# Value bias folded into the value weight, and the f1 bias products placed behind the first attention, in an attention and feed-forward kernel on one core

## Chip, cores and metric

One core of a Trainium2 chip runs the kernel. The metric is the device time of one execution in microseconds; less is better. Engines are named as in the profile: PE is TensorE (matmuls), DVE is VectorE, ACT is ScalarE, POOL is GpSimd, SP issues the loads and stores.

## What is computed

The input x is 8 batches of 512 rows of 256 numbers. The reference, cut down:

```python
x = x + attn_block(layernorm(x), ...)
x = x + ffn_block(layernorm(x), W_fc, ln_w, ln_b, W_proj)

# attn_block
x_norm = layer_norm(x, ln1_w, ln1_b)
Q = elu(x_norm @ q_w.T + q_b) + 1;  K = elu(x_norm @ k_w.T + k_b) + 1     # 64 features each
V = x_norm @ v_w.T + v_b
# causal, step by step in n: KV += k v^T ; Ks += k ; out = (q KV) / (q . Ks + 1e-6)
x = x + (attn @ o_w.T + o_b)
h = gelu(layer_norm(x, ln2_w, ln2_b) @ f1_w.T + f1_b)                      # 1024 wide
x = x + h @ f2_w.T + f2_b

# ffn_block: W_fc and W_proj are rounded to -1, 0, 1 by their mean absolute value
h = layernorm(gelu(x @ absmean(W_fc).T)) * ln_w + ln_b
return h @ absmean(W_proj).T
```

## The kernel before

**Precision.** Most products are made in fp32r from a high and a low part of each operand: hi x hi, hi x lo, lo x hi (split3). The high part is a copy on ACT (names ending in _hi), the low part a subtraction on DVE (_lo). wfc and wpj hold -1, 0, 1 and need no low part.

**One batch g** (T = 4 row tiles of 128, h or half = two of them, k = two column tiles of D = 256):

- ln1_stats, ln1_rstd (POOL), ln1_shift, u_norm: u, the normalised row. tu flips it (four 128x128 transposes per half) and u_hi, u_lo copy it to uT.
- qk_mm, then qk_max, qk_exp (its own ACT table), qk_sum, qk_hi, k_dup, qk_lo make q_stack, k_stack and k_lo. scores makes the causal blocks in three banks; ae_mask, ad_mask, af_mask multiply the diagonals; the parts go to ae, ad, af.
- v_mm multiplies uT by wvo, the product of v_w, o_w and ln1_w, so attend gives rows of the output projection at once. v has 258 columns: column 256 is one, so that attend sums up the denominator too. attend(g, t) starts each sum with ones_row x eps_row, which adds 1e-6 to the denominator and takes 1e-6 times the bias row from the others. attn_out divides and adds xa, which holds n1 (the row normalised for the inner residual) plus bo_b: POOL's n1o adds it.
- ln2, z2_norm, tz2, z2_hi, z2_lo; f1(g, m), m = 0..7, each 128 of the 1024 wide layer, gelu, h_hi, h_lo; f2(g, m) sums them up; y_sum.
- ln3, z3_norm, tz3, z3_hi, z3_lo; fc(g, t, c), gelu3; tr flips h3, g_hi and g_lo apply ln_w; proj; correct (POOL) and output; store.

**Order.** Each engine has its instructions written out as a list: first() for batch 0, step(g) for batches 1 to 5, last() for 6 and 7. A step interleaves work of batches g-1, g, g+1 and g+2. Engines run their lists in order and wait for each other by semaphores (pe.wait_ge and so on). Nothing reorders them, so a place in a list is a place in time.

**Set-up in first().** wqk and wvo are scaled by ln1_w. qkb multiplies ln1_b by the raw q and k weights; bvo makes the bias row of v and o, from the columns vb and ln1_b spread over 128 columns by wide_cols: bo_rows adds o_b to it (bo_b) and makes eps_raw, which eps_split and eps_lo turn into eps_row. f1b makes the bias of f1 from ln2_b: 16 products of one column each, into bank_y[0]; f1_bias_add adds f1_b, and gelu(0, 0) waits for that. abs_part(0..3), theta_sum, threshold and ternary make wfc and wpj from the raw weights. In SP's list the load of the raw fc waits for wf1_lo, and the load of the raw pj, into the place where f1_raw lay, waits for f1b:

```python
            sp.wait_ge(s["wf1_lo"], 4)
            sp.dma_start(fc_raw, fc_d).then_inc(s["fc_loaded"], 16)
            sp.wait_ge(s["f1b_done"], 1)
            sp.dma_start(pj_raw, pj_d).then_inc(s["pj_loaded"], 16)
```

Of the kernel before, what the change touches and what calls it, by code (L numbers as in the profile page):

```python
# [1301 lines left out]
```

## Time and profile before

| | |
|---|---|
| runs | 467.3, 467.65, 470.79 us, median 467.65 |
| profiled execution | 467.8 us, its span (first to last instruction) 465.8 us |
| PE busy | 448.6 us, 96% of the span |
| DVE, ACT, POOL busy | 369.0, 322.3, 187.5 us |
| mean granted clock of PE | 0.985 of full |

A share of busy time is a mean over the whole span. PE's matmuls overlap: the distance from one start to the next is what a matmul costs in a packed row, and is shorter than the duration of its record. A granted clock of 1.00 is 2.4 GHz and 0.50 is 1.2 GHz. Lines (L346) are those of the kernel before.

### The profile page before, as it was taken

How to read it: one execution, taken by the hardware profiler on the slowest of the kernel's cores; microseconds unless marked ns; L12 is line 12 of the kernel's file. 1: busy time of each engine (PE TensorE's matmuls, PEld its weight loads, DVE VectorE, ACT ScalarE, POOL GpSimd, SP SyncE). 2: the span in 40 equal slices, each digit the busy share in tenths (PEclk: the TensorE clock that was granted, in tenths of full speed). 3: DMA queues.
4: the chain of work that ended last, by engine and by line, in shares of the span. 5: the costliest groups of instructions: out<-in, count | busy, mean ns of one | idle time of the engine just before them, and what ended most of it. 6: DMA issues, size and time to landing. Idle time of an engine off the chain costs nothing.

```text
span 465.8 us, 8944 instructions
## 1 busy us (share of the span) xinstructions
PE 448.6 (96%) x3012; PEld 408.1 (88%) x3012; DVE 369.0 (79%) x1184; ACT 322.3 (69%) x606; POOL 187.5 (40%) x188
## 2 busy tenths in 40 slices
PE   4988999999999999999999999999999999999996
PEld 4876898889989999889989899889998999889875
DVE  6978969875898779985898868986898768767675
ACT  4976856988368864988468874788459793775262
POOL 3967025510565042640545123740545323540433
PEclk9977999999999999999999999999999999999999
DMA  7241000000020002000020002000020000000001
GB/s 236 117 181 45 1 2 1 1 23 2 1 68 2 25 0 69 2 23 1 2 68 2 24 0 70 0 24 2 1 68 2 23 1 15 9 2 24 0 23 46
DMA packets 10044, 14.08 MB, mean 30 GB/s; under 512 B 784, under 2 KB 9104, under 8 KB 9488
## 3 DMA queue, kind: packets, MB, share of 16 engines
q1 hardware_dynamic: 10000, 13.52, 8.6%
q8 instruction: 24, 0.39, 0.4%
q14 instruction: 20, 0.16, 0.1%
HBM read 9.32 MB, written 4.19 MB: 29 GB/s over the span
## 4 chain that ended last, share of the span: by engine, by line
PE 69%; issue 13%; POOL 6%; DVE 2%; ACT 1%; POOLq 0%; DVEq 0%; ACTq 0%
PE bank_f L415 10%; PE bank_p L445 10%; PE bank_f L203 5%; PE bank_f L204 5%; PE bank_f L205 5%; PE bank_y L204 5%; PE bank_y L203 5%; PE bank_y L205 5%; PE bank_y L429 4%; PE bank_a L203 3%; PE bank_a L205 3%; PE bank_a L204 3%; PE bank_a L211 2%; PE bank_f L211 1%; POOL rs L1155 1%
## 5 line engine op out<-in xcount | busy, mean ns | idle before, releaser
L1155 POOL TENSOR_TENSOR rs<-ve,neg_half 128x2 f32<-128x2 f32 x48 | 33.7, 701 | 227.3 <-DVE ve L846 225.5
L204 PE MATMUL bank_y<-wf_lo,h_hi 128*128 128x256 f32 x240 | 67.1, 280 | 0.0
L203 PE MATMUL bank_y<-wf_hi,h_hi 128*128 128x256 f32 x240 | 67.1, 279 | 0.0
L205 PE MATMUL bank_y<-wf_hi,h_lo 128*128 128x256 f32 x240 | 67.0, 279 | 0.0
L445 PE MATMUL bank_p<-wpj_t,g_hi 128*128 128x256 f32 x256 | 64.0, 286 | 0.3 <-DVE y_yc L1048 0.3
L445 PE MATMUL bank_p<-wpj_t,g_lo 128*128 128x256 f32 x256 | 62.4, 280 | 0.0
L1039 DVE SCALAR_TENSOR_TENSOR g_lo<-bank_y,vec,g_hi 128x256 fp32r<-128x256 f32 x128 | 54.9, 477 | 9.4 <-ACT g_hi L687 9.2
L687 ACT ACTIVATE g_hi<-bank_y,vec 128x256 fp32r<-128x256 f32 x128 | 52.5, 475 | 10.2 <-PE bank_y L429 8.2
L650 ACT ACTIVATE bank_f<-bank_f,f_bias 128x512 f32<-128x512 f32 x64 | 42.3, 660 | 23.7 <-PE bank_f L205 23.2
L415 PE MATMUL bank_f<-wfc_t,z3T_hi 128*128 128x512 f32 x128 | 53.9, 421 | 1.4 <-DVE z3T_lo L907 1.4
L203 PE MATMUL bank_f<-z2T_hi,wf_hi 128*128 128x512 f32 x128 | 53.3, 416 | 1.2 <-DVE z2T_lo L907 1.2
L907 DVE TENSOR_TENSOR h_lo<-bank_f,h_hi 128x512 fp32r<-128x512 f32 x60 | 41.2, 686 | 15.2 <-ACT h_hi L658 14.9
L678 ACT ACTIVATE h<-bank_f 128x512 f32<-128x512 f32 x64 | 38.3, 600 | 20.0 <-PE bank_f L415 19.8
L205 PE MATMUL bank_f<-z2T_hi,wf_lo 128*128 128x512 f32 x128 | 51.4, 402 | 0.0
L204 PE MATMUL bank_f<-z2T_lo,wf_hi 128*128 128x512 f32 x128 | 51.4, 402 | 0.0
L415 PE MATMUL bank_f<-wfc_t,z3T_lo 128*128 128x512 f32 x128 | 50.6, 396 | 0.0
L445 PEld LDWEIGHTS bank_p<-wpj_t,g_hi 128*128 128x128 f32 x256 | 48.1, 188 | 1.8 <-issue 0.5
L445 PEld LDWEIGHTS bank_p<-wpj_t,g_lo 128*128 128x128 f32 x256 | 48.3, 189 | 1.0
L203 PEld LDWEIGHTS bank_y<-wf_hi,h_hi 128*128 128x128 f32 x240 | 45.2, 188 | 1.1
L204 PEld LDWEIGHTS bank_y<-wf_lo,h_hi 128*128 128x128 f32 x240 | 45.1, 188 | 1.0
L205 PEld LDWEIGHTS bank_y<-wf_hi,h_lo 128*128 128x128 f32 x240 | 45.1, 188 | 0.0
L1025 DVE BATCH_NORM_STATS2 bn<-h 128x6 f32<-128x512 f32 x64 | 41.1, 681 | 1.6 <-ACT h L678 1.5
(293 smaller groups left out, 1209.5 us busy)
## 6 DMA issues: line engine op xcount, KB each, us to landing
out<-y_yc SPq DMA_DIRECT2D x16, 256.0 KB, 2.2
x_even<-in_x SPq DMA_DIRECT2D x8, 256.0 KB, 3.0
x_odd<-in_x SPq DMA_DIRECT2D x8, 256.0 KB, 3.1
h<-in_f SPq DMA_DIRECT2D x1, 1024.0 KB, 7.9
y_yc<-in_f SPq DMA_DIRECT2D x1, 1024.0 KB, 9.9
h<-in_fc SPq DMA_DIRECT2D x1, 1024.0 KB, 4.9
h<-in_pj SPq DMA_DIRECT2D x1, 1024.0 KB, 4.8
z<-in_wv SPq DMA_DIRECT2D x1, 256.0 KB, 4.0
```

The source lines that it names most:

```text
L203: pe.matmul(ps, w[0], r[0], start=start, stop=False, skip_group_check=skip)
L204: pe.matmul(ps, w[0], r[1], start=False, stop=False, skip_group_check=skip)
L205: return pe.matmul(ps, w[1], r[0], start=False, stop=stop, skip_group_check=skip)
L415: mm = pe.matmul(bank_f[c][:], z3T[part][:, k, t * P:(t + 1) * P], wfc[:, k, c * 512:(c + 1) * 512], start=(k == 0 and part == 0), stop=(k ...
L445: mm = pe.matmul(bank_p[:, t * D:(t + 1) * D], gr[part][:, (8 * g + 4 * h + q) % RG, i, t * P:(t + 1) * P], wpj[:, m, :], start=(m == 0 an ...
L650: act.activation(bank_f[m % 2][:], bank_f[m % 2][:], ACT.Gelu, bias=f1_bias[:, m:m + 1]).then_inc(s["h_gelu"], 1)
L678: act.activation(h3[:, t, c * 512:(c + 1) * 512], bank_f[c][:], ACT.Gelu).then_inc(s["h3_ready"], 1)
L687: act.activation(gr[0][:, n % RG, i, :], bank_y[q % 2][:, i * D:(i + 1) * D], ACT.Copy, scale=ln3w_c[:, m:m + 1]).then_inc(s["g_hi"], 1)
L907: dve.tensor_tensor(dst, b, hi.bitcast(F32), ALU.subtract).then_inc(s[ready], 1)
L1025: dve.bn_stats(bn[3][:, t, 6 * c:6 * c + 6], h3[:, t, c * 512:(c + 1) * 512]).then_inc(s["ln4_bn"], 1)
L1039: dve.scalar_tensor_tensor(gr[1][:, n % RG, i, :], bank_y[q % 2][:, i * D:(i + 1) * D], ln3w_c[:, m:m + 1], gr[0][:, n % RG, i, :].bitcast ...
L1155: pool.tensor_tensor(rs[n][:, 2 * h:2 * h + 2], ve[n][:, 2 * h:2 * h + 2], neg_half[:, 0:2], ALU.pow).then_inc(s[f"ln{n + 1}_rs"], 1)
```

## The change

The sum of a normalised row u is zero. If one is added to each element of u, its product with a matrix that has the same row b/D in each of its D rows is b. So the bias of v and o is put into wvo, and uT holds u + 1: u_hi copies with a bias of one, u_lo adds one before it subtracts. The added one also brings the column sums of the weights; for q and k, and within wvo, these are taken out again by less_w = ln1_b - ln1_w in the place of ln1_b. With the bias in v, attention's numerator holds it, and 1e-6 is added to the denominator by itself:

- ones_row, eps_row, eps_hi, eps_raw, bo_b, eps_split, bo_rows and eps_lo are gone, and the matmul ones_row x eps_row that began each attend.
- attn_out has a new step den = b[:, D] + 1e-6, and the reciprocal waits for it.
- n1o adds ob_b, as loaded. A new dcol makes less_w; qkb and wide_cols wait for it.
- wvo_hi is split: wvo_copy copies the raw product, then bvo, then wvo_add (DVE) scales it and adds the bias row, then wvo_hi and wvo_lo.
- f1b stands behind attend(0, 3), v_mm(0) behind scores(0), and the lists of all engines are written in another order.

```diff
-                    mm = pe.matmul(bank_a[0][:, 0:1], wqk_raw[:, k, :], ln1b_c[:, k:k + 1],
+                    mm = pe.matmul(bank_a[0][:, 0:1], wqk_raw[:, k, :], less_w[:, k:k + 1],
...
                 b = a_bank(g, (2, 0, 1, 2)[t])
-                pe.matmul(b[:, 0:VW], ones_row[:], eps_row[:], start=True, stop=False)
...
-                    mm = split3(b[:, 0:VW], w, [r[:, j, :] for r in v], False, j == t)
+                    mm = split3(b[:, 0:VW], w, [r[:, j, :] for r in v], j == 0, j == t)
...
-                qkb(); tu(0, 0); tu(0, 1); wvo_mm(); qk_mm(0); bvo(); v_mm(0, 0); v_mm(0, 1); scores(0); f1b()
-                attend(0, 0); attend(0, 1); attend(0, 2); tu(1, 0); attend(0, 3); tu(1, 1); tz2(0, 0); tz2(0, 1)
+                qkb(); tu(0, 0); tu(0, 1); wvo_mm(); qk_mm(0); bvo(); scores(0); v_mm(0, 0); v_mm(0, 1)
+                attend(0, 0); attend(0, 1); attend(0, 2); attend(0, 3); f1b(); tz2(0, 0); tz2(0, 1); tu(1, 0)
...
+            def wvo_copy():
+                act.wait_ge(s["wvo_done"], 1)
+                act.activation(wvo_raw.rearrange("p k d -> p (k d)"), bank_a[1][:], ACT.Copy).then_inc(s["wvo_copied"], 1)
+
             def wvo_hi():
...
+                act.wait_ge(s["wvo_sum"], 2)
+                act.activation(wvo[0][:].rearrange("p k d -> p (k d)"), bank_a[1][:], ACT.Copy).then_inc(s["wvo_hi"], 1)
...
-                act.activation(uT[0][:, :, 2 * h * P:(2 * h + 2) * P], by_k(a_bank(g, h)), ACT.Copy).then_inc(s["u_hi"], 1)
+                else:
+                    act.wait_ge(s["one_set"], 1)
+                act.activation(uT[0][:, :, 2 * h * P:(2 * h + 2) * P], by_k(a_bank(g, h)), ACT.Identity,
+                               bias=one[:]).then_inc(s["u_hi"], 1)
...
+            def wvo_add():
+
+                dve.wait_ge(s["bvo_done"], 1)
+                dve.wait_ge(s["vec_loaded"], 16)
+                for k in range(KD):
+                    dve.scalar_tensor_tensor(bank_a[1][:, k * D:(k + 1) * D], wvo_raw[:, k, :], ln1w_c[:, k:k + 1],
+                                             bank_q[:, 0:D], ALU.mult, ALU.add).then_inc(s["wvo_sum"], 1)
...
-                lo_part(uT[1][:, :, cols], by_k(a_bank(g, h)), uT[0][:, :, cols], "u_lo")
+                dve.scalar_tensor_tensor(uT[1][:, :, cols], by_k(a_bank(g, h)), 1.0, uT[0][:, :, cols].bitcast(F32),
+                                         ALU.add, ALU.subtract).then_inc(s["u_lo"], 1)
...
-                dve.reciprocal(rden[:, t:t + 1], b[:, D:D + 1]).then_inc(s["rden_ready"], 1)
+                dve.tensor_scalar(den[:, t:t + 1], b[:, D:D + 1], 1.0, ATTN_EPS, ALU.mult, ALU.add).then_inc(s["den_ready"], 1)
+                dve.wait_ge(s["den_ready"], 4 * g + t + 1)
+                dve.reciprocal(rden[:, t:t + 1], den[:, t:t + 1]).then_inc(s["rden_ready"], 1)
```

PE, the start of batch 0, before: bvo (bank_a<-z,xa and bank_a<-xa), v_mm (bank_y<-wvo, 24 rows), scores (q_stack), f1b (bank_y<-vec,h), the first attend.

```order
L236 MATMUL bank_a<-z,xa 128x256 x2
L236 MATMUL bank_a<-xa 128x256 x2
L203 MATMUL bank_y<-wvo_hi,uT_hi 128x256
L204 MATMUL bank_y<-wvo_lo,uT_hi 128x256
...
L311 MATMUL bank_f<-q_stack,k_stack 128x512
L312 MATMUL bank_f<-q_stack,k_lo 128x512
...
L245 MATMUL bank_y<-vec,h 128x1 x16
L346 MATMUL bank_p<-eps_row,ones_row 128x258
L203 MATMUL bank_p<-v_hi,ae_hi 128x258
```

The same place now; behind f1b (L243) stand tz2(0) (bank_f<-ident,z), tu(1) (bank_a<-ident,u) and theta_sum(0).

```order
L234 MATMUL bank_a<-z,xa 128x256 x2
L234 MATMUL bank_a<-xa 128x256 x2
L308 MATMUL bank_f<-q_stack,k_stack 128x512
...
L201 MATMUL bank_y<-wvo_hi,uT_hi 128x256
...
L201 MATMUL bank_p<-v_hi,ae_hi 128x258
...
L243 MATMUL bank_y<-vec,h 128x1 x16
L209 MATMUL bank_f<-ident,z 128x128 x8
L209 MATMUL bank_a<-ident,u 128x128 x8
L254 MATMUL bank_y<-abs_sum,mean_w 128x2
L201 MATMUL bank_f<-z2T_hi,wf_hi 128x512
```

v_mm moved behind scores, f1b behind the attends, tu(1) behind tz2(0), and the row with eps_row is gone.

ACT between the second layer norm of batch 0 and its first gelus, before: z2_norm, z2_hi, abs_part(2) and (3) (g_hi,abs_sum<-h), gelu with its table load (bank_f), h_hi.

```order
L558 ACTIVATE z<-xa,sh,rs 128x256 x2
L643 ACTIVATE z2T_hi<-bank_f 128x2x256 x2
L541 ACTIVATE g_hi,abs_sum<-h 128x1024 x2
L650 ACT_TABLE_LOAD
L650 ACTIVATE bank_f<-bank_f,f_bias 128x512
L658 ACTIVATE h_hi<-bank_f 128x512
```

And now:

```order
L546 ACTIVATE z<-xa,sh,rs 128x256 x2
L634 ACTIVATE z2T_hi<-bank_f 128x2x256 x2
L580 ACTIVATE uT_hi<-bank_a,one 128x2x256 x2
L529 ACTIVATE g_hi,abs_sum<-h 128x1024
L641 ACT_TABLE_LOAD
L641 ACTIVATE bank_f<-bank_f,f_bias 128x512
```

u_hi(1) came in ahead of abs_part(2), and abs_part(3) went behind the second gelu.

DVE in a middle batch, behind the second v_lo (v_lo<-bank_a), before: output (y_yc<-bank_p), ln3_shift(g, 1) (sh<-mv,rs), attn_out(g + 1, 0) and ln2_stats (bn<-xa), z3_lo.

```order
L907 TENSOR_TENSOR v_lo<-bank_a,v_hi 128x2x256
L1048 SCALAR_TENSOR_TENSOR y_yc<-bank_p,rs,y_yc 128x256 x2
L852 TENSOR_SCALAR sh<-mv,rs 128x1 x2
L968 RECIPROCAL rden<-bank_a 128x1
L971 SCALAR_TENSOR_TENSOR xa<-bank_a,rden,xa 128x256
L976 BN_STATS bn<-xa 128x6
L907 TENSOR_TENSOR z3T_lo<-bank_f,z3T_hi 128x2x256
```

And now:

```order
L896 TENSOR_TENSOR v_lo<-bank_a,v_hi 128x2x256
L841 TENSOR_SCALAR sh<-mv,rs 128x1 x2
L1040 SCALAR_TENSOR_TENSOR y_yc<-bank_p,rs,y_yc 128x256 x2
L958 TENSOR_SCALAR den<-bank_a 128x1
L960 RECIPROCAL rden<-den 128x1
```

The ln3_shift went ahead of output, and den stands ahead of each reciprocal.

## Rows read from the trace of the kernel before

**Rows 1.** The page, busy us of each engine, share of the span, instructions.

```profile
PE 448.6 (96%) x3012; PEld 408.1 (88%) x3012; DVE 369.0 (79%) x1184; ACT 322.3 (69%) x606; POOL 187.5 (40%) x188
```

**Rows 2.** Three stretches, one batch each: us, busy us (records) by engine, clock, loads.

```profile
236.26:289.53 53.27, 53.27 (x369) 48.98 (x369) 43.47 (x142) 38.77 (x73) 21.28 (x21) 1.00 0.07 22
```

**Rows 3.** TensorE's waits: us in total, times, longest.

```profile
PE bank_f L211 <- ACT z L558: 2.4, 1, 2.4
PE bank_f L415 <- DVE z3T_lo L907: 1.4, 1, 1.4
...
PE bank_a L346 <- DVE v_lo L907: 0.5, 1, 0.5
```

**Rows 4.** TensorE in order of time, two attends: start us, us, instruction.

```profile
286.88 0.28 PE L346 MATMUL bank_a<-eps_row,ones_row 128*128 128x258 f32 x1
287.00 0.29 PE L203 MATMUL bank_a<-v_hi,ae_hi 128*128 128x258 f32 x1
```

**Rows 5.** TensorE in order of time, batch 0.

```profile
15.28 1.03 PE L236 MATMUL bank_a<-xa 128*128 128x256 f32 x4
...
19.54 0.50 PE L311 MATMUL bank_f<-q_stack,k_stack 128*128 128x512 f32 x1
...
20.93 5.27 PE L245 MATMUL bank_y<-vec,h 128*128 128x1 f32 x32
26.11 0.55 PE L346 MATMUL bank_p<-eps_row,ones_row 128*128 128x258 f32 x1
...
32.20 0.60 PE L211 MATMUL bank_a<-ident,u 128*128 128x128 f32 x4
...
38.96 0.79 PE L203 MATMUL bank_f<-z2T_hi,wf_hi 128*128 128x512 f32 x1 [1.20 <-DVE z2T_lo L907]
...
43.74 0.28 PE L256 MATMUL bank_p<-abs_sum,mean_w 128*128 128x2 f32 x2
...
45.37 0.40 PE L203 MATMUL bank_f<-z2T_hi,wf_hi 128*128 128x512 f32 x1
```

**Rows 6.** Stretches of half a us: TensorE's granted clock is the third last number.

```profile
22.50:23.00 0.50, 0.50 (x5) 0.50 (x5) 0.50 (x3) 0.50 (x2) 0.29 (x1) 0.65 0.00 0
...
36.00:36.50 0.50, 0.04 (x1) 0.07 (x2) 0.50 (x2) 0.50 (x2) 0.50 (x2) 0.80 0.00 0
43.00:43.50 0.50, 0.50 (x3) 0.43 (x2) 0.25 (x1) 0.22 (x1) 0.50 (x1) 0.87 0.08 25
```

**Rows 7.** ACT in order of time, and the load of pj (us to landing).

```profile
39.31 1.06 ACT L541 ACTIVATE g_hi<-h 128x1024 fp32r<-128x1024 f32 x1
...
40.48 1.28 ACT L650 ACT_TABLE_LOAD   x1
41.92 0.66 ACT L650 ACTIVATE bank_f<-bank_f,f_bias 128x512 f32<-128x512 f32 x1 [0.17 <-PE bank_f L205]
...
h<-in_pj SPq DMA_DIRECT2D x1, 1024.0 KB, 4.8
```

**Rows 8.** DVE in a middle batch, and the f1 of TensorE behind it.

```profile
287.19 0.16 DVE L968 RECIPROCAL rden<-bank_a 128x1 f32<-128x1 f32 x1
287.38 0.48 DVE L971 SCALAR_TENSOR_TENSOR xa<-bank_a,rden,xa 128x256 f32<-128x256 f32 x1
...
290.19 0.69 DVE L907 TENSOR_TENSOR z3T_lo<-bank_f,z3T_hi 128x512 fp32r<-128x512 f32 x1 [0.22 <-ACT z3T_hi L669]
...
301.37 0.88 DVE L1039 SCALAR_TENSOR_TENSOR g_lo<-bank_y,vec,g_hi 128x256 fp32r<-128x256 f32 x2 [0.31 <-ACT g_hi L687]
302.27 0.69 DVE L907 TENSOR_TENSOR z2T_lo<-bank_a,z2T_hi 128x512 fp32r<-128x512 f32 x1
...
303.34 0.48 PE L203 MATMUL bank_f<-z2T_hi,wf_hi 128*128 128x512 f32 x1
```

**Rows 9.** ACT and TensorE ahead of the scores of a middle batch.

```profile
324.33 2.08 ACT L558 ACTIVATE xa<-x_even,sh,rs 128x256 f32<-128x256 f32 x4
...
325.27 0.40 PE L311 MATMUL bank_a<-q_stack,k_stack 128*128 128x512 f32 x1
```

More of the change, by code:

```diff
@@ L323, in v_mm @@
                     pe.wait_ge(s["u_lo"], h + 1)
-                    pe.wait_ge(s["wvo_lo"], 2)
+                    pe.wait_ge(s["wvo_lo"], 1)
                 for j in range(2):
@@ L690, in first @@
             def first():
-                tables(); wqk_hi(); u_norm(0, 0); u_norm(0, 1); u_hi(0, 0); u_hi(0, 1); ln3_hi(); wf1_hi(0)
-                wf1_hi(1); wvo_hi(); wf1_hi(2); qk_exp(0); wf1_hi(3); qk_hi(0); wf2_hi(0); k_dup(0); v_hi(0, 0)
-                n1(0); ad_hi(0); ae_hi(0); v_hi(0, 1); af_hi(0); eps_split(); u_norm(1, 0); wf2_hi(1); wf2_hi(2)
-                abs_part(0); u_norm(1, 1); u_hi(1, 0); abs_part(1); u_hi(1, 1); wf2_hi(3); z2_norm(0, 0)
-                z2_norm(0, 1); z2_hi(0, 0); z2_hi(0, 1); abs_part(2); abs_part(3); gelu(0, 0); h_hi(0, 0)
@@ new lines, in first @@
+                tables(); u_norm(0, 0); u_norm(0, 1); u_hi(0, 0); u_hi(0, 1); wqk_hi(); wf1_hi(0); wf1_hi(1)
+                ln3_hi(); wvo_copy(); wf1_hi(2); qk_exp(0); wf1_hi(3); qk_hi(0); wvo_hi(); k_dup(0); n1(0); af_hi(0)
+                ad_hi(0); v_hi(0, 0); ae_hi(0); v_hi(0, 1); wf2_hi(0); wf2_hi(1); u_norm(1, 0); wf2_hi(2); wf2_hi(3)
+                u_norm(1, 1); abs_part(0); abs_part(1); z2_norm(0, 0); z2_norm(0, 1); z2_hi(0, 0); z2_hi(0, 1)
+                u_hi(1, 0); u_hi(1, 1); abs_part(2); gelu(0, 0); h_hi(0, 0); gelu(0, 1); h_hi(0, 1); abs_part(3)
@@ L1051, in first @@
             def first():
-                consts(); ln1_stats(0, 0); ln1_stats(0, 1); ln1_shift(0, 0); u_odd(0, 0); ln1_shift(0, 1)
-                u_odd(0, 1); n1_ve(0); u_lo(0, 0); n1_shift(0); selectors(); u_lo(0, 1); wide_cols(); wqk_lo()
-                ln1_stats(1, 0); qk_bias_add(); qk_max(0); wvo_lo(); qk_sum(0); ln1_stats(1, 1); qk_lo(0)
-                v_lo(0, 0); ln3_lo(); n1_ve(1); ad_mask(0); ae_mask(0); bo_rows(); af_mask(0); ad_lo(0)
-                ln1_shift(1, 0); ae_lo(0); af_lo(0); eps_lo(); v_lo(0, 1); attn_out(0, 0); ln2_stats(0, 0)
@@ new lines, in first @@
+                consts(); ln1_stats(0, 0); ln1_stats(0, 1); dcol(); ln1_shift(0, 0); u_odd(0, 0); ln1_shift(0, 1)
+                n1_ve(0); u_odd(0, 1); u_lo(0, 0); wide_cols(); wqk_lo(); n1_shift(0); u_lo(0, 1); qk_bias_add()
+                ln1_stats(1, 0); qk_max(0); qk_sum(0); wvo_add(); selectors(); ln1_shift(1, 0); qk_lo(0); wvo_lo()
+                ln1_stats(1, 1); af_mask(0); ad_mask(0); ae_mask(0); af_lo(0); ad_lo(0); v_lo(0, 0); ae_lo(0)
+                v_lo(0, 1); attn_out(0, 0); ln2_stats(0, 0); attn_out(0, 1); ln1_shift(1, 1); attn_out(0, 2)
@@ new lines, in first @@
+                af_mask(1); ln1_stats(2, 1); h_lo(0, 7); n1_ve(2); af_lo(1); ae_lo(1); ad_lo(1); y_sum(0, 0)
+                ln3_stats(0, 0); y_sum(0, 1); v_lo(1, 0); ln3_stats(0, 1); ln3_shift(0, 0); v_lo(1, 1)
+                ln3_shift(0, 1); attn_out(1, 0); ln2_stats(1, 0); attn_out(1, 1); ln1_shift(2, 0); z3_lo(0, 0)
+                z3_lo(0, 1); ln2_stats(1, 1); attn_out(1, 2); ln2_var(1, 0); attn_out(1, 3); ln2_stats(1, 2)
+                ln2_shift(1, 0); ln2_stats(1, 3); ln2_var(1, 1); ln4_stats(0, 0); g_lo(0, 0, 0); ln2_shift(1, 1)
```

286 lines of the change are left out of this document (128 added, 158 removed).

## The prediction

> **What bounds the kernel now.** I read the busy line first, then three equal batches, TensorE's waits, the order in time of TensorE, and last what DVE, ACT and the loads do at the places that the change touches. TensorE is busy 96% of the span [rows 1]. In a middle batch it is busy 53.27 of 53.27 us with 369 matmul records, while DVE has 43.47 and ACT 38.77 [rows 2]: in batches 1 to 6 the time is the sum of TensorE's start-to-start distances. It waits only at the two ends and behind batch 0: for the first loads, 2.4 us for the second layer norm of batch 0, 1.4 us for the first z3 [rows 3]. So an edit pays if it takes matmuls out of the packed part, or if it shortens the start up to the point where the packed part begins. The profiled execution took 467.8 us for a span of 465.8, against a median of 467.65 of three runs (467.3 to 470.79), so savings in the span can be taken from the median as they are.
>
> **The epsilon products.** Each attend began with ones_row x eps_row, 128x258. In the packed part it starts at 286.88 and the next at 287.00: 0.12 us, although a record alone shows 0.28 [rows 4]. Four go in each of 8 batches. Those of batches 1 to 7: 28 x 0.12 = 3.4 us, all on the path. The four of batch 0 are in the start, below. Other matmuls only change places, and a packed engine pays the same sum for them.
>
> **What DVE gets for it.** Each attn_out has a den step of one column, then a wait, then the reciprocal. No such step is in the trace of before; the nearest is the reciprocal, 0.16 us busy and 0.19 to the step that waits for it [rows 8]. Bounds 0 to 0.48 (its 256-wide neighbour); I take 0.19, 0.76 per batch. DVE has 53.27 - 43.47 = 9.8 us of idle per batch, so the sum is covered, but the stretch from attn_out to z2_lo is nearly full: z2_lo ends at 302.96 and the f1 that waits for it starts at 303.34, cover 0.38 [rows 8]. The new order takes n1_ve, an ln1_shift and an ln3_shift out of that stretch, eight one-column steps that do not wait for one another; at half the reciprocal's 0.16 each, an estimate, that is some 0.7 us, so den is about paid back, while TensorE comes 4 x 0.12 = 0.48 earlier. DVE also waited 0.22 and 0.31 us for ACT in the stretch, time that can be used. I take no wait, with 0.36 us per batch (rival 2) as its bound. u_hi with a bias and u_lo with an added constant keep their shapes: nothing, hidden in ACT's and DVE's idle time.
>
> **The start, to f1(0,2), the first work after which TensorE of before never waits until f2 ends (45.37 [rows 5]).**
> a) v_mm(0) used to stand between bvo and scores(0), and filled the time from about 16.3 to 19.2 in which qk is made. Now wvo_hi and wvo_lo wait for bvo, so v_mm stands behind scores. TensorE is empty from 16.3 (bvo, [rows 5]) until qk_lo. qk_lo comes some 0.3 later than for the 19.54 of before, since wvo_add, selectors and a shift stand ahead of it on DVE: scores at 19.85.
> b) scores take 1.39 (19.54 to 20.93 [rows 5]), v_mm 24 x 0.12 = 2.9: 4.3 us at full clock. But TensorE is empty for 3.5 us before. In the trace the clock fell at 36.4, after a 2.4 us wait and a shorter one with only four transposes between, and was back at 43.1, 4.1 us after dense work began at 38.96 [rows 3, 5, 6]. So I take the clock as lost here as well, at 1.2 GHz for some 3.4 us of this work, which costs half of it: +1.7. v_mm ends at 25.85.
> c) The first attend waits for masks and v_lo: 0.5. Its 30 matmuls x 0.12 = 3.6 run at full clock, where before the clock had fallen at 22.8 in f1b, ahead of them [rows 6]. End of attention 30.0, against 32.2, the start of the tu behind it [rows 5].
> d) f1b comes now: 5.2 us (20.93 to 26.11 [rows 5]), one column each, to 35.2. It lies under the DVE-POOL-ACT chain of the second layer norm, which needed 3 us in before, 32.2 to 35.2; so f1b itself is late by some 2 us.
> e) Two things hang on f1b. The load of pj is issued behind it, as in before, and lands 4.8 us later [rows 7]: 40.1. ACT has abs_part(2), which reads it, ahead of gelu(0,0): 1.2 (39.31 to the table load at 40.48), the table load 1.3, gelu 0.7 [rows 7], h_hi and h_lo about the same each, 0.4 for the hand-overs: 5.0. f1(0,2) waits for h_lo(0,0): 45.1. On the other branch tz2, 16 transposes and theta start at 35.2, f1(0,0) near 39.1; the twelve matmuls of f1(0,0) and f1(0,1) took 4.8 in before (38.96 to 43.74 [rows 5]), and qk_mm 1.5 (to 45.37, less theta), which gives 45.4, or 43.5 if the 16 transposes bring the clock back earlier. I take the pj branch, 45.1; gain **0.3**, bounds -0.3 and +1.9 (clock kept).
>
> **Behind it.** theta_sum(1) moves from before f1(0,2) to behind it: -0.2. From f2's end of batch 0 to fc(0,0,1) before had the waits 0.5 and 1.4 [rows 3]; now the third attend stands ahead of tz3 and waits for the second v_lo. I add the same DVE steps in the new order, and come to waits of 0.6 and 0.9, but one fc less lies under them: -0.2. At the end fc(7,0,0), which filled the wait for the last tz3, stands behind it, and z3_lo behind output(6,1): -0.2. Sum 3.4 + 0.3 - 0.2 - 0.2 - 0.2 = **3.1 us**: span 462.7, profiled execution 464.7, median 464.5.
>
> **Rule and row.** In b) the trace of before has no single wait of 3.5 us in the middle of work, only two shorter ones. The Trainium skill (TensorE: Matmul & The Clock Gate, "HAM oscillation") says that waits between stretches of matmuls put the clock back to half each time, and that one should keep TensorE fed. That speaks against this change, which opens such a wait where there was none. By it b) stands, 464.5; if the short waits of the rows were needed together, 462.9. No row of before shows this wait alone. The same page (What's actually happening) has the clock follow how busy TensorE is; the row differs: from 22.5 to 23.0 TensorE was busy 0.50 of 0.50 us, in f1b, and the clock fell [rows 6].
>
> **Rivals.**
> 1. The clock is kept over the empty stretch: b) costs nothing, attention ends at 28.3, f1b 33.5, pj 38.4, f1(0,2) 43.5, gain 1.9 instead of 0.3: **462.9**. For: scores start soon after. Against: the length of the gap. Chance 0.24.
> 2. DVE closes the ring in each batch: den's 0.76 is not paid back and z2_lo is late by 0.76 + 0.48 - 0.38 - 0.5 = 0.36, six times 2.2 us: **466.7**. For: cover of 0.38. Against: 9.8 us of idle. Chance 0.15.
> 3. The other side: ACT now has n1(g+1), 2.08 us, ahead of qk_hi and k_dup, where it stood behind k_dup (324.33, just as k_dup ended). scores started at 325.27, so cover was 0.96 [rows 9]. qk_exp goes ahead of h_hi(4), and f2 pieces ahead of scores, and by my sum of the new order about 0.5 us of cover is left. If those moves don't help, scores wait 2.08 - 0.96 = 1.1 us in each of six batches, 6.7 us: **471.2**, over before by 3.5. It turns slower than before from 0.52 us per batch on. Chance 0.07.
> 4. The change doesn't do what it says: a start of 258 columns taken out only lets the next one wait for its weights, and nothing of the 3.4 comes back: **467.9**. Against: the records follow at 0.12 with their loads beneath. Chance 0.04.
>
> **How the numbers follow.** Forecast 0.50, rivals 0.24, 0.15, 0.07 and 0.04. The range runs from 462.2 (rival 1 with the small losses gone) to 467.0 (rival 2); outside are rival 3, rival 4 and the ends, under 0.2. One per cent, 4.7 us, is about what this measurement can tell from no change: faster by more is 462.97 or less. Rival 1 lies on that line, 0.16 of its 0.24; the forecast gives 0.08: faster 0.24. Slower 0.05 from rival 3, the rest 0.71 within.
>
> **What would show it.** Right: no ones_row records; a middle batch of 52.8 us with TensorE busy throughout; an empty TensorE of about 3.5 us before scores(0) and half clock after it; f1b between attend(0,3) and tz2(0,0); abs_part(2) waiting for the pj load, near 40; f1(0,2) near 45. Wrong: a batch of 53 us or more (rivals 2 to 4, by the wait that stands at f1, scores or nowhere), or f1(0,2) near 43.5 at full clock. A clock lost for longer, or the wait for pj growing with its load, would move the start by more than my bounds.

## The result, and the profile after

The changed kernel takes 463.83 us, the median of 11 runs (462.61 to 464.79), against 469.58 for 11 runs of the kernel before (467.3 to 471.42): a ratio of 0.9881, 95% interval 0.9859 to 0.9904. The first three runs of before, on which the prediction rests, had a median of 467.65; it forecast 464.5. The time is 0.7 us off. The gain is further off: 3.1 us was forecast, 4.7 us lie between the spans of the two profiled executions (465.8 and 461.1), and 5.75 between the two medians of 11. The part in the packed batches is the one that was forecast. The rest came in the start, for which 0.3 us had been put down.

The page of the changed kernel, busy us by engine [rows 1], and a middle batch, from f1(4,0) to f1(5,0), in the columns of [rows 2]:

```profile
PE 441.1 (96%) x2980; PEld 399.3 (87%) x2980; DVE 369.7 (80%) x1212; ACT 321.1 (70%) x603; POOL 185.7 (40%) x188
```

```profile
247.02:299.81 52.79, 52.79 (x368) 48.23 (x366) 43.74 (x148) 38.66 (x74) 21.23 (x21) 1.00 0.07 21
```

A batch takes 52.79 us where it took 53.27: 0.48 less, four times 0.12, with TensorE busy throughout as before. The 32 records of ones_row are gone, and nothing has taken their place in the packed part.

TensorE in order of time in batch 0, the rows that answer to [rows 5]:

```profile
14.93 1.03 PE L234 MATMUL bank_a<-xa 128*128 128x256 f32 x4
20.30 0.50 PE L308 MATMUL bank_f<-q_stack,k_stack 128*128 128x512 f32 x1 [4.34 <-DVE k_lo L896]
...
26.86 0.36 PE L201 MATMUL bank_p<-v_hi,ae_hi 128*128 128x258 f32 x1 [0.63 <-DVE v_lo L896]
...
30.53 3.63 PE L243 MATMUL bank_y<-vec,h 128*128 128x1 f32 x32
34.44 0.84 PE L209 MATMUL bank_f<-ident,z 128*128 128x128 f32 x4 [0.28 <-ACT z L546]
...
38.42 0.48 PE L201 MATMUL bank_f<-z2T_hi,wf_hi 128*128 128x512 f32 x1
...
43.59 0.50 PE L201 MATMUL bank_f<-z2T_hi,wf_hi 128*128 128x512 f32 x1 [0.70 <-DVE h_lo L896]
```

The empty stretch is there, 4.34 us long. scores(0) start at 20.30, the first attend at 26.86, attention ends at 30.53, and f1b stands where the prediction put it. But it takes 3.63 us instead of 5.27 [rows 5]. The last row is f1(0,2): 43.59, where before had 45.37, and it waits 0.70 us for h_lo.

The granted clock at the same places (third last number of a row, as in [rows 6]):

```profile
21.00:21.50 0.50, 0.50 (x5) 0.50 (x4) 0.50 (x2) 0.00 (x0) 0.50 (x2) 0.63 0.00 0
24.50:25.00 0.50, 0.50 (x6) 0.50 (x6) 0.00 (x0) 0.16 (x1) 0.50 (x2) 0.96 0.00 0
31.00:31.50 0.50, 0.50 (x7) 0.50 (x6) 0.43 (x3) 0.50 (x1) 0.00 (x0) 1.00 0.00 0
34.50:35.00 0.50, 0.50 (x4) 0.38 (x4) 0.46 (x3) 0.28 (x1) 0.50 (x1) 0.79 0.00 0
38.00:38.50 0.50, 0.50 (x6) 0.50 (x4) 0.20 (x1) 0.45 (x2) 0.50 (x2) 0.80 0.52 213
```

A stretch with 0.63 has 0.13 us at full and the rest at half. So behind the empty stretch the clock is at half (1.2 GHz) from 21.1 to 24.5, 3.4 us, as forecast. It is at full (2.4 GHz) in all of f1b, falls at 34.8, and is back at 38.2, just ahead of f1(0,0). Read in the same way, it was at half in before from 22.7 to 29.5 and from 36.3 to 43.1, 6.8 us each time.

**Where the 4.7 us lie**, as distances between the same instructions in the two traces:

| stretch | before | after | gain | forecast |
| --- | --- | --- | --- | --- |
| start of the span to f1(0,2) | 45.37 | 43.59 | 1.78 | 0.3 |
| f1(0,2) to f1(1,0) | 44.91 | 45.08 | -0.17 | 0.08 (0.48 - 0.2 - 0.2) |
| five middle batches | 266.33 | 263.92 | 2.41 | 2.4 |
| f1(6,0) to the end of the span | 109.19 | 108.51 | 0.68 | 0.28 (0.48 - 0.2) |

The waits behind the start, first of before, then of after:

```profile
72.20 0.39 PE L346 MATMUL bank_a<-eps_row,ones_row 128*128 128x258 f32 x1 [0.49 <-DVE v_lo L907]
...
443.28 0.50 PE L415 MATMUL bank_f<-wfc_t,z3T_hi 128*128 128x512 f32 x1 [1.41 <-DVE z3T_lo L907]
```

```profile
70.57 0.39 PE L201 MATMUL bank_a<-v_hi,ae_hi 128*128 128x258 f32 x1 [0.49 <-DVE v_lo L896]
...
72.67 0.39 PE L201 MATMUL bank_a<-v_hi,ae_hi 128*128 128x258 f32 x1 [0.74 <-DVE v_lo L896]
...
436.42 0.66 PE L209 MATMUL bank_f<-ident,z 128*128 128x128 f32 x4 [0.76 <-ACT z L546]
437.57 0.50 PE L410 MATMUL bank_f<-wfc_t,z3T_hi 128*128 128x512 f32 x1 [0.49 <-DVE z3T_lo L896]
```

The third attend of batch 1 waits 0.74 us for the second v_lo, which is new. The 1.41 us wait for z3T_lo in before lay at 443.28, in batch 7, and not behind batch 0, where the prediction used it.

In a middle batch DVE and ACT stand to TensorE like this; the rows of the first block answer to [rows 8], those of the second to [rows 9]:

```profile
283.90 0.15 DVE L958 TENSOR_SCALAR den<-bank_a 128x1 f32<-128x1 f32 x1
284.08 0.17 DVE L960 RECIPROCAL rden<-den 128x1 f32<-128x1 f32 x1
...
298.90 0.69 DVE L896 TENSOR_TENSOR z2T_lo<-bank_a,z2T_hi 128x512 fp32r<-128x512 f32 x1 [0.41 <-ACT z2T_hi L634]
...
299.81 0.48 PE L201 MATMUL bank_f<-z2T_hi,wf_hi 128*128 128x512 f32 x1
```

```profile
322.05 0.63 ACT L598 ACTIVATE k_stack<-k_stack 64x512 fp32r<-64x512 f32 x1
...
323.13 0.39 PE L308 MATMUL bank_a<-q_stack,k_stack 128*128 128x512 f32 x1
```

A den step costs 0.18 us to the reciprocal (0.19 taken). k_dup ends at 322.68, 0.45 us ahead of the scores that need it (0.5 forecast). z2_lo ends at 299.59, 0.22 ahead of f1.

### The profile page after: what moved, and what is told of

The parts are those of the page before. It is cut to its first block, busy times and chain, and to the rows that moved or that the text cites. A ratio compares the mean times of both kernels' runs of the same rounds, so it can differ in the third digit from the quotient of the medians.

```text
span 461.1 us, 8907 instructions
## 1 busy us (share of the span) xinstructions
PE 441.1 (96%) x2980; PEld 399.3 (87%) x2980; DVE 369.7 (80%) x1212; ACT 321.1 (70%) x603; POOL 185.7 (40%) x188
## 4 chain that ended last, share of the span: by engine, by line
PE 84%; DVE 6%; issue 4%; POOL 2%; ACT 2%; DMA 1%; DVEq 0%; POOLq 0%; ACTq 0%
PE bank_f L410 13%; PE bank_p L440 12%; PE bank_y L201 6%; PE bank_y L202 6%; PE bank_y L203 6%; PE bank_f L201 6%; PE bank_f L203 6%; PE bank_y L424 6%; PE bank_f L202 6%; PE bank_a L201 4%; PE bank_a L203 4%; PE bank_a L202 4%; PE bank_a L209 3%; PE bank_f L209 2%; PE bank_a L308 1%
## 5 line engine op out<-in xcount | busy, mean ns | idle before, releaser
L669 ACT ACTIVATE h<-bank_f 128x512 f32<-128x512 f32 x64 | 38.7, 607 | 21.2 <-PE bank_f L410 21.1
L202 PEld LDWEIGHTS bank_y<-wf_lo,h_hi 128*128 128x128 f32 x240 | 45.1, 188 | 0.9
L201 PEld LDWEIGHTS bank_y<-wf_hi,h_hi 128*128 128x128 f32 x240 | 45.1, 188 | 0.9
L203 PEld LDWEIGHTS bank_y<-wf_hi,h_lo 128*128 128x128 f32 x240 | 45.1, 188 | 0.0
```

The source lines that it names most:

```text
L201: pe.matmul(ps, w[0], r[0], start=start, stop=False, skip_group_check=skip)
L202: pe.matmul(ps, w[0], r[1], start=False, stop=False, skip_group_check=skip)
L203: return pe.matmul(ps, w[1], r[0], start=False, stop=stop, skip_group_check=skip)
L669: act.activation(h3[:, t, c * 512:(c + 1) * 512], bank_f[c][:], ACT.Gelu).then_inc(s["h3_ready"], 1)
```

## The experiments

Twelve kernels. A batch is the distance from one f1(g,0) to the next; f1(0,2) is read from TensorE's order in time. Since the moment at which the clock falls shifts from run to run (the mean clock of the runs of after is 0.985 to 0.993, of before 0.982 to 0.989), the start is read with its clock beside it, and what is said of the clock below holds for the one execution of each kernel that was traced.

### The products of ones, put back

eps_row holds zeros here; the 1e-6 still comes from the den step.

```
+ if g:
+     pe.matmul(b[:, 0:VW], ones_row[:], eps_row[:], start=True, stop=False)
- mm = split3(..., j == 0, j == t)
+ mm = split3(..., j == 0 and g == 0, j == t)
```

> The changed kernel with one 128x258 product of ones by zeros put back at the head of each attend of batches 1 to 7 (the epsilon still comes from the den step). Theory: each costs 0.12 us of the packed TensorE, 28 of them 3.4 us; a middle batch takes 53.27 us again instead of 52.79, and the span is 464.5 instead of 461.1. Rival (the product was hidden, and the time went elsewhere): batch stays at 52.79 and the span at 461.1.

Measured: 468.79 us, ratio to before 1.0 (0.9983 to 1.0017), span 467.1; a batch took 53.47:

```profile
251.00:304.47 53.47, 53.47 (x372) 48.95 (x370) 43.77 (x148) 38.63 (x74) 21.20 (x21) 1.00 0.07 21
```

More than either expected. In the attends the sum was right: three batches gave 1.43 us more there, 0.48 per batch. The rest was in f2, whose 279 matmul distances had a mean of 119.6 ns instead of 116.8 in the same three batches, and in proj (122.2 instead of 120.0) and v_mm (113.3 instead of 119.9, which is faster). Behind f1(0,2) the kernel took 4.3 us more than after, the products included; another 1.7 us came in the start (f1(0,2) at 45.29), where the clock was at half twice for 6.8 us and not twice for 3.4. The two tensors had been declared in the middle of the others and had moved the addresses behind them. So the same again with the two at the end:

```
  few_rows = sb("few_rows", [4, 2 * P + D])
+ ones_row = sb("ones_row", [P, P], F32R)
+ eps_row = sb("eps_row", [P, VW], F32R)
```

> The kernel with the 28 products of ones by zeros put back, as in the run before, but with their two tensors declared behind all others, so that every other tensor keeps the address that it has in the changed kernel. With the tensors in the middle a batch took 53.47 us: 0.48 in the attends, and the rest in f2, whose matmuls followed each other at 119.7 ns instead of 116.8. Theory (the 0.12 per product is the cost, the rest came from moved addresses): f2 back at 116.8 ns, batch 53.27 us. Rival (the products themselves slow f2, or make some wait longer): batch 53.47 again.

Measured: 466.33 us, ratio 0.9953 (0.9929 to 0.9977), span 464.3, f2 at 116.8 ns, and

```profile
248.79:302.06 53.27, 53.27 (x371) 48.71 (x370) 43.78 (x148) 38.65 (x74) 21.20 (x21) 1.00 0.06 21
```

Its start agrees with that of after within 0.12 us (f1(0,2) at 43.71), so this is the clean measurement of the term: 0.48 us per batch, and 464.3 - 461.1 = 3.2 us of span for 28 products, with one wait behind batch 0 that is 0.23 shorter (0.51 instead of 0.74). The 3.4 us was right, rival 4 is out, and so is the rival expected for this run: f2 went back to its pace.

### More steps for DVE

```
  dve.wait_ge(s["den_ready"], 4 * g + t + 1)
+ if g:
+     for r in range(2):
+         dve.tensor_scalar(den[:, t:t + 1], den[:, t:t + 1], 1.0, 0.0, ALU.mult, ALU.add)  # each waits for the last
```

> The changed kernel with two more dependent one-column steps behind den in each attn_out of batches 1 to 7: 2 x 0.19 x 4 = 1.5 us more on DVE per batch. z2_lo(g,1) ended 0.22 us before f1(g,0) started, and DVE waited 0.41 us for ACT in the stretch ahead of it. Theory (DVE is close to closing the ring): 1.5 - 0.22 - 0.41 = 0.9 us or less per batch comes through, a middle batch of 53.0 to 53.7 us, span 463 to 467. Rival (the 9 us of idle DVE time cover it): batch 52.79, span 461.1.

Measured: 467.52 us, ratio 0.9972 (0.9957 to 0.9987), span 464.8; batches of 53.22, 53.25, 53.25, 53.38 and 53.24 us. One attend's steps on DVE:

```profile
286.35 0.34 DVE L962 TENSOR_SCALAR den<-den 128x1 f32<-128x1 f32 x2
286.73 0.16 DVE L964 RECIPROCAL rden<-den 128x1 f32<-128x1 f32 x1
```

The pair costs 0.38, four of them 1.52 per batch, and 0.48 of it comes out on TensorE. So 1.0 us of cover was left in each batch beyond den's own 0.76. Rival 2 had the right mechanism, the ring through DVE does close, but its point lies a good microsecond further off than the 0.36 it charged.

### f1b ahead of attention again

```
- attend(0, 0); attend(0, 1); attend(0, 2); attend(0, 3); f1b(); tz2(0, 0)
+ f1b(); attend(0, 0); attend(0, 1); attend(0, 2); attend(0, 3); tz2(0, 0)
```

> The changed kernel with f1b ahead of attend(0,0) instead of behind attend(0,3), and nothing else. f1b then waits for v_lo(0,0), takes 3.6 us at full clock from 26.5 and lies on the path ahead of attention, and the empty time behind attention is open again. Theory (the start gains because f1b covers the chain of the second layer norm): attention ends at 34.1 instead of 30.5, tz2(0,0) comes 3.6 us later and f1(0,2) near 46.5 instead of 43.6, span 463.5 to 464.5. Rival (the place of f1b doesn't matter, only the clock does): f1(0,2) within 0.5 us of 43.6, span 461.1.

Measured: 469.24 us, ratio to before 0.9995 (0.9968 to 1.0021): all that the change had gained is lost by this one move. The ten runs lie between 466.74 and 470.47 at mean clocks of 0.989 to 0.977, and the traced one (469.82) is among the longest: span 468.1, f1(0,2) at 50.66, 7.1 us later than in after, where 3 had been expected. TensorE's wait and the clock:

```profile
41.40 1.12 PE L209 MATMUL bank_f<-ident,z 128*128 128x128 f32 x4 [3.62 <-ACT z L546]
```

```profile
29.00:29.50 0.50, 0.50 (x6) 0.50 (x6) 0.00 (x0) 0.50 (x2) 0.50 (x1) 1.00 0.63 246
30.00:30.50 0.50, 0.50 (x4) 0.50 (x4) 0.00 (x0) 0.50 (x2) 0.50 (x2) 0.50 0.00 0
36.50:37.00 0.50, 0.50 (x5) 0.50 (x4) 0.50 (x2) 0.50 (x1) 0.00 (x0) 0.72 0.00 0
```

The wait of 3.62 us for the second layer norm is the open gap that was expected. On top of it the clock fell at 29.95, in f1b, and stayed at half until 36.8, under most of attention. That is the pattern of the kernel before: f1b, then attention at half clock. In all it was at half for 20.5 us before f1(0,2) (also from 19.7 to 26.5 and from 40.2 to 47.0), where after has 6.8.

### One part alone: before, with f1b moved behind attention

```
- scores(0); f1b() ... attend(0, 3); tu(1, 1); tz2(0, 0)
+ scores(0)        ... attend(0, 3); tu(1, 1); f1b(); tz2(0, 0)
```

(and DVE's f1_bias_add behind z2_odd(0,1))

> The kernel before with one part of the change alone: f1b stands behind attend(0,3) and tu(1,1), ahead of tz2(0,0), and DVE adds the bias behind z2_odd(0,1). In before f1b lay under the chain of masks and v_lo, which ended at 26.6, so attention can't start much before 25. Theory: f1b at full clock takes 3.6 us under the 3 us chain of the second layer norm, attention runs faster only as far as the clock is full there; f1(0,2) comes 0.5 to 1.5 us earlier than 45.4, span 464.3 to 465.3 against 465.8. Rival (moving f1b alone gives all of the 1.8 us at the start): f1(0,2) at 43.6. Other rival (it needs v_mm behind scores): f1(0,2) at 45.4 or later.

Measured: 470.14 us, ratio to before 1.0012 (0.9989 to 1.0034), span 468.4, f1(0,2) at 47.82. The second rival: the move alone gives nothing.

```profile
26.23 0.56 PE L346 MATMUL bank_p<-eps_row,ones_row 128*128 128x258 f32 x1 [4.52 <-DVE eps_row L785]
```

```profile
25.19 0.80 DVE L785 TENSOR_TENSOR eps_row<-eps_raw,eps_hi 1x258 fp32r<-1x258 f32 x1
26.01 0.69 DVE L907 TENSOR_TENSOR v_lo<-bank_y,v_hi 128x512 fp32r<-128x512 f32 x1
```

With v_mm still ahead of scores, the masks and the epsilon row are DVE's, and attention cannot start before 26.2 wherever f1b stands. TensorE waits 4.52 us for them, the clock falls in that wait at 24.4, and attention runs at half. f1b itself, at full clock behind attention, took 3.63 us here too, and then held up ACT. It ended at 37.16, the load of pj went out at 37.20, and both abs_part steps that read it stand ahead of gelu in this kernel:

```profile
42.05 1.06 ACT L541 ACTIVATE g_hi<-h 128x1024 fp32r<-128x1024 f32 x1 [3.26 <-DMA h<-in_pj]
```

f1(0,2) waited 1.11 us for h_lo behind that. Without the wait TensorE would have come to it at 46.71, still 1.3 us later than in before. So neither part gives the gain alone: f1b late is not enough in before, and the rest of the change is not enough with f1b early. That it is v_mm behind scores that makes f1b free for the other gap, by filling the time in which DVE does the masks, is read from the rows; no run moved v_mm by itself.

### What the empty stretch costs: a filler of one column, and a wide one

Between bvo and scores(0), where TensorE is empty, 16 products that nobody reads, first f1b's own shape, one column each:

```
+ def fill():   # f1b's loop, into bank_a0
- bvo(); scores(0)
+ bvo(); fill(); scores(0)
```

> The changed kernel with 16 matmuls of one column that nobody reads (f1b's, into the free bank_a0) between bvo and scores(0), where TensorE is empty from 16.0 to 20.3; the real f1b stays behind attention. Theory (the empty stretch puts the clock to half in scores and v_mm): the filler ends near 19.7, scores start at 20.3 as now, the clock stays at full from there to the end of v_mm, which ends at 24.6 instead of 26.1; f1(0,2) 1 to 1.5 us earlier than 43.6, span 459.6 to 460.1. Rival (the clock falls anyway, as it fell in before in the middle of busy f1b): same clock, f1(0,2) at 43.6 or later.

Measured: 463.62 us, ratio 0.9881 (0.9834 to 0.9928), span 461.3, f1(0,2) at 43.85. No gain, and at first sight the rival:

```profile
15.99 3.63 PE L253 MATMUL bank_a<-vec,h 128*128 128x1 f32 x32
```

```profile
18.00:18.50 0.50, 0.50 (x7) 0.50 (x6) 0.50 (x2) 0.47 (x2) 0.48 (x1) 1.00 0.00 0
21.50:22.00 0.50, 0.50 (x4) 0.50 (x3) 0.47 (x3) 0.00 (x0) 0.50 (x1) 0.50 0.00 0
```

TensorE was busy 0.50 of 0.50 us in the stretch, waited 0.87 us behind it for k_lo, and the clock fell in scores just the same. In the run with f1b in the same stretch (the last one below) the clock fell at 18.6, inside f1b, with no wait between. Then with products of 256 columns, `pe.matmul(bank_a[0][:, 0:256], wqk_hi, uT_hi[:, 0:256])`, 34 times (the row below stops at 33, where its view ends):

> The changed kernel with 34 products 128x256 that nobody reads between bvo and scores(0), 0.12 us each, where TensorE is empty from 16.0 to 20.3. The filler of one-column matmuls there kept TensorE busy, and the clock still fell, at 21.5, for 3.3 us. Theory (what counts is dense work of many columns): the clock stays at full through scores and v_mm, v_mm ends at 24.6, f1(0,2) 1 to 1.5 us earlier than 43.6, span 459.6 to 460.1. Rival (the clock falls at this point whatever TensorE does): a fall of some 3.3 us between 18 and 22 again, span 461 to 462.

```profile
15.93 4.27 PE L250 MATMUL bank_a<-uT_hi,wqk_hi 128*128 128x256 f32 x33
```

```profile
24.00:24.50 0.50, 0.50 (x6) 0.50 (x6) 0.50 (x2) 0.50 (x2) 0.50 (x1) 1.00 0.00 0
32.00:32.50 0.50, 0.50 (x5) 0.50 (x5) 0.47 (x6) 0.22 (x2) 0.07 (x1) 0.68 0.00 0
```

Measured: 462.16 us, ratio 0.9837 (0.9784 to 0.9891), span 460.6. The clock stays at full through scores and v_mm, and the first attend comes at 25.75 instead of 26.86, in spite of scores that start 0.34 later. So step b) is right: the empty stretch costs 3.4 us at half clock, 1.7 us of work. But of that only 0.46 arrives at f1(0,2) (43.13), where 1 to 1.5 had been expected: the clock then falls at 32.2, in f1b, and is at half until 39.0. f1b takes 4.32 us, the load of pj goes out behind it, and ACT waits:

```profile
38.59 1.06 ACT L534 ACTIVATE g_hi<-h 128x1024 fp32r<-128x1024 f32 x1 [0.42 <-DMA h<-in_pj]
```

f1(0,2) waited 0.47 us for h_lo behind that.

### f1b 64 columns wide

The last run asks that of f1b itself. The same column is used 64 times, and DVE reads the first; DVE's order is that of the kernel with selectors() moved (below).

```
- pe.matmul(bank_y[0][:, m:m + 1], f1_raw[...], ln2b_c[:, k:k + 1], ...)
+ pe.matmul(bank_y[0][:, 64 * m:64 * m + 64], f1_raw[...], ln2b_c[:, k:k + 1].to_broadcast([P, 64]), ...)
```

> The kernel with selectors() and the shift behind wvo_lo(0) (alone: 461.65 us median, span 459.9), and f1b's 16 matmuls made 64 columns wide, the same column 64 times, of which DVE reads the first. So far f1b, TensorE busy throughout but one column wide, had the clock fall in it or within 1 us behind it in every run, and 34 wide products in the empty stretch kept the clock where 16 narrow ones did not. Theory (one-column products count as nearly idle): f1b takes 3.6 to 4.5 us, the clock is at full through f1b and falls, if at all, only for a wait behind it; f1(0,0) at full clock, f1(0,2) at 42.0 to 42.6, median 460.5 to 461.7. Rival (the width doesn't matter): the clock falls between 29 and 33 and is at half until 36 to 40, median 461.7 or more.

Measured: 462.0 us, ratio 0.9848 (0.9814 to 0.9881), span 460.0.

```profile
29.53 3.68 PE L243 MATMUL bank_y<-vec,h 128*128 128x64 f32 x32
...
42.53 0.50 PE L201 MATMUL bank_f<-z2T_hi,wf_hi 128*128 128x512 f32 x1 [1.24 <-DVE h_lo L896]
```

```profile
33.00:33.50 0.50, 0.26 (x3) 0.12 (x2) 0.50 (x7) 0.39 (x1) 0.50 (x2) 1.00 0.00 0
36.00:36.50 0.50, 0.39 (x5) 0.30 (x3) 0.43 (x1) 0.50 (x3) 0.50 (x1) 1.00 1.08 459
```

The 64 columns take no longer than one (3.68 us), and the clock does not fall at all behind f1b, not even in the waits of 0.24, 0.67 and 0.42 us up to f1(0,0), which starts at 36.81 and runs at full. In the traces of the other eleven kernels and of both originals the clock was at half somewhere between 30 and 38. The runs that were not traced bear this out only in part: the mean clock was 0.996 or 1.0 in four of the six runs of this kernel, and in the eight runs of the two kernels with the same order of DVE ahead of attention and a narrow f1b (selectors() moved, abs_part(2) moved) it was 0.987 to 0.993 in seven and 0.996 in one. The time did not follow the theory, which had 460.5 to 461.7: no run was below 461.68, against 461.65 for the narrow f1b in the same order, and f1(0,2) waits 1.24 us for h_lo. Behind h_lo stand gelu, its table and abs_part(2), and that waits for pj:

```profile
37.99 1.06 ACT L529 ACTIVATE g_hi<-h 128x1024 fp32r<-128x1024 f32 x1 [0.81 <-DMA h<-in_pj]
...
39.17 1.28 ACT L641 ACT_TABLE_LOAD   x1
```

It is the branch of step e) of the prediction, the load of pj issued behind f1b. It shows once TensorE is fast: 0.42 us in the run with the wide filler, 0.81 here.

### Four other orders of the start

selectors() (1.6 us at this place, 0.6 in before and 0.6 where it is moved to; why is not shown) and a shift of 0.3 us stand on DVE ahead of q_lo and k_lo. Moved behind:

```
- wvo_add(); selectors(); ln1_shift(1, 0); qk_lo(0); wvo_lo()
+ wvo_add(); qk_lo(0); wvo_lo(); selectors(); ln1_shift(1, 0)
```

> The changed kernel with selectors(), 1.6 us on DVE, and the shift of ln1(1,0), 0.3 us, behind wvo_lo(0) instead of ahead of qk_lo(0). Theory (DVE's order holds scores(0) back): q_lo starts at 17.0, k_lo at 17.6; scores(0) wait for k_dup, which ended at 18.7, and start at 18.8 instead of 20.3; everything up to f1(0,2) comes 1.2 to 1.5 us earlier, span 459.6 to 459.9. Rival (v_lo and the masks, or abs_part(2) and its table, are next to limit): f1(0,2) less than 0.6 us earlier.

Measured: 461.65 us (461.61 to 461.75, 4 runs), ratio to before 0.9838 (0.9793 to 0.9882), span 459.9.

```profile
19.01 0.79 PE L308 MATMUL bank_f<-q_stack,k_stack 128*128 128x512 f32 x1 [2.94 <-DVE k_lo L896]
```

scores(0) come 1.29 us earlier, f1(0,2) 1.03 (42.56). By its median this is the fastest of all the kernels here, and none of its runs overlaps with those of after (462.61 to 464.79). Both were timed against before and not against each other, and the intervals of their ratios overlap.

With 23 wide products in what is left of the gap:

> Both together: selectors() and the shift behind wvo_lo(0) (alone 459.9 us span, scores(0) at 19.0), and 23 wide products that nobody reads in the empty stretch, 16.0 to 18.8. If the wide filler keeps the clock: v_mm ends 1.7 us earlier, span 458.2 to 458.6. If it doesn't: 459.9 as without.

Measured: 462.26 us, ratio 0.9851 (0.9795 to 0.9907), span 460.3. The clock was kept through v_mm, but the first attend waited 1.49 us for v_lo, which needs ACT and DVE, and the clock fell again at 32.3, 0.2 us behind the narrow f1b. With abs_part(2) behind h_hi(0,1) on ACT instead of the filler:

> selectors() and the shift behind wvo_lo(0), and on ACT abs_part(2), 1.2 us, behind h_hi(0,1) instead of ahead of gelu(0,0), with no filler. Theory (abs_part(2) stands on the path to f1(0,2) when the clock is full in f1(0,0)): the 0.7 us wait for h_lo goes, f1(0,2) up to 0.7 us earlier, span 459.2 to 459.9; where the clock is at half in f1(0,0), as in the run with selectors alone, nothing. Rival (theta and the ternary weights come too late then, and cpj or fc waits): span over 460.

Measured: 462.36 us, ratio 0.9842 (0.9796 to 0.9888), span 460.6. No gain (f1(0,2) at 42.83, 0.27 later than with selectors() alone): the clock was at half in f1(0,0) (until 39.3), and there was no wait for h_lo to take away. It was tried with the narrow f1b only; with the wide one, where the wait is 1.24 us, it remains open.

And f1b itself put into the empty stretch (in bank_a0, its bias added ahead of the masks), with tu(1,0) and tu(1,1) ahead of tz2(0,0), and selectors() at its place of after:

```
- bvo(); scores(0) ... attend(0, 3); f1b(); tz2(0, 0); tz2(0, 1); tu(1, 0); tu(1, 1)
+ bvo(); f1b(); scores(0) ... attend(0, 3); tu(1, 0); tu(1, 1); tz2(0, 0); tz2(0, 1)
```

> The changed kernel with the real f1b in the empty stretch between bvo and scores(0), in bank_a0, the bias added by DVE before the masks, and tu(1,0), tu(1,1) ahead of tz2(0,0). Theory (f1b costs nothing there, and LN2's chain is then the limit behind attention): attention ends at 29.3, tz2(0,0) starts 33.3, f1(0,0) 36.0, pj lands early; f1(0,2) near 41.5 or as h_lo(0,0) allows, span 459 to 459.5. Rival (the empty 3 us behind attention put the clock to half again for f1(0,0) and f1(0,1)): f1(0,2) at 43 to 44, span 461.

Measured: 464.23 us, ratio 0.9893 (0.9846 to 0.994), span 462.3: the rival, and worse than it said. f1(0,2) came at 44.94, where it had 43 to 44.

```profile
18.50:19.00 0.50, 0.50 (x5) 0.50 (x5) 0.47 (x4) 0.47 (x2) 0.50 (x1) 0.63 0.00 0
25.00:25.50 0.50, 0.50 (x4) 0.50 (x4) 0.10 (x1) 0.00 (x0) 0.50 (x1) 0.54 0.00 0
```

```profile
35.26 0.74 PE L209 MATMUL bank_f<-ident,z 128*128 128x128 f32 x4 [2.76 <-ACT z L546]
```

f1b costs nothing in the gap, but the clock fell in it at 18.6 and was at half until 25.5, and again from 35.7 to 42.5, behind the 2.76 us wait that f1b no longer covers. Twice 6.8 us at half clock, where after has twice 3.4.

## Why the prediction was right, and where it was not

**The epsilon products: right.** 0.12 each, 0.48 per batch, 2.41 over five batches, and undone by the products alone (53.27 us per batch). The den steps cost DVE what was said and no wait; the cover was larger than I had worked out.

**a) scores(0) at 19.85: right in kind, 0.45 off.** They came at 20.30. selectors() took 1.6 us on DVE, where it had taken 0.6 in before; the run with it and a shift moved shows that they were on the path, for 1.3 us.

**b) The clock lost over the empty stretch: right.** 3.4 us at half, as taken, and the wide filler took them away. The Trainium skill (TensorE: Matmul & The Clock Gate, "HAM oscillation") has a wait between stretches of matmuls put the clock back; after and the run with the wide filler agree with it (4.34 us empty and 3.4 us at half, against none). Rival 1, which had the clock kept here, was wrong, though its time of 462.9 and its f1(0,2) at 43.5 lie close to what was measured.

**c) Attention ends at 30.0: 30.53**, with the delay of a).

**d) f1b takes 5.2 us: this is the step that failed.** The row of before is 32 records in one sum, 5.27 us, and I took 0.165 each as its price. But the clock fell inside it, at 22.7. The rows of before show it by their counts (the first number in brackets is TensorE's records in half a us):

```profile
21.00:21.50 0.50, 0.50 (x7) 0.50 (x7) 0.50 (x3) 0.50 (x2) 0.44 (x1) 1.00 0.00 0
...
23.00:23.50 0.50, 0.50 (x4) 0.50 (x4) 0.50 (x2) 0.50 (x2) 0.44 (x1) 0.50 0.00 0
```

Seven at full clock and four at half. At full the 32 take 3.63 us (0.113 each), as after and six experiments have it within 0.01; in before 1.7 us ran at full and 3.5 at half, and 1.7 + 3.5 / 2 is 3.5. I had priced an instruction at a clock at which it would not run, though I had cited that very fall.

**e) What hangs on f1b.** With f1b 1.6 us shorter than its price, less the 0.5 of a) and c), the load of pj went out at 34.19 instead of 35.2 and was there when ACT came to it:

```profile
39.07 1.05 ACT L529 ACTIVATE g_hi<-h 128x1024 fp32r<-128x1024 f32 x1
...
40.23 1.28 ACT L641 ACT_TABLE_LOAD   x1
```

I had said that abs_part(2) would wait for the load, near 40.1. No wait stands there: it starts at 39.07, right behind u_hi. The path was still ACT's, since f1(0,2) waits 0.70 us for h_lo, and from abs_part(2) to f1(0,2) it took 4.52 us where my sum had 5.0. So of the 1.5 us by which f1(0,2) came sooner than 45.1, 1.0 is f1b, with which the load ceased to hold ACT up, and 0.5 the chain behind it. The other branch, which I had put at 45.4, or 43.5 if the transposes bring the clock back in time, went the second way: the clock was back at 38.2, and TensorE would have come to f1(0,2) at 42.89. The gain of 1.78 lies just inside my bound of 1.9, which I had kept for another cause.

Two of the signs that I had named came out against me: abs_part(2) did not wait, and f1(0,2) was near 43.5 at full clock, which I had put down as a sign of being wrong. The half clock behind the empty stretch shows that rival 1 was not what brought it there. So the mechanism of the start was in the prediction, and its size was 1.5 us short.

**Behind the start** I had read the 1.41 us wait for z3T_lo as lying behind batch 0. It lies in batch 7 ([rows 3] give totals and no times). Behind batch 0 the waits grew from 0.49 to 1.23, -0.74 and not -0.2; in batch 7 those from 0.27 + 1.41 + 0.16 + 0.28 = 2.12 fell to 0.76 + 0.49 + 0.62 = 1.87, +0.25 and not -0.2. Two errors of the same origin that nearly cancel: of the sum, 0.65 was lost to f1(1,0) against 0.4, and 0.2 gained at the end.

**Rivals.** 2: den had 1.0 us of cover to spare. 3: k_dup ended 0.45 us ahead of scores, as forecast, and no batch waited. 4: fell with the products put back.

The median of before over 11 runs is 1.9 us above that of its first three, so the change looks larger in medians (5.75 us) than between the two traces (4.7); in the runs of before the mean granted clock is 0.982 to 0.989, in those of after 0.985 to 0.993. That this is the same effect, a later or earlier fall of the clock in the start, is what the spans suggest; it was not traced in the longer runs. In part it was luck that the median came within 0.7 us of 464.5: the forecast was taken from a median of before that was 1.9 us low, and its gain was 2.65 us too small against the medians of 11.

## What to carry to other kernels

A group that sums many records has no price until it is split by the granted clock: count its records in a stretch at full and in one at half, and price the moved instruction at the clock it will run at. A wait in a list without times must be looked up in the order of time before it is put to a place. And f1b, which covered a wait for the path, did not cover it for the clock: in after the clock fell 0.6 us behind its 3.63 us. Whether the time saved arrives is decided by the next wait, here v_lo, then the load of pj.
